# Product-key scatter on one NeuronCore: two f16 parts in one 64-column matmul, combined on three engines

## The reference, cut to what matters

```python
s, i = jax.lax.top_k(sim, k)                  # 8 best of 64 keys, for two halves x and y of the key
all_scores = (sx[..., :, None] + sy[..., None, :]).reshape(b, n, h, k * k)
all_idx = (ix[..., :, None] * nk + iy[..., None, :]).reshape(b, n, h, k * k)
scores, pk = jax.lax.top_k(all_scores, k)     # 8 best of the 64 pairs, for each of 8 heads
idx = jnp.take_along_axis(all_idx, pk, axis=-1)
o = jnp.einsum('bnd,bnhkd->bnhk', inputs, key_in[idx])
o = jax.nn.gelu(o) * jax.nn.softmax(scores, axis=-1)
return jnp.einsum('bnhk,bnhkd->bnd', o, key_out[idx])
```

## Time and profile before

| | |
|---|---|
| median of 3 runs | 3328.03 us (3327.47 to 3328.57) |
| profiled execution | 3329.2 us, its span 3327.3 us |
| TensorE busy | 3090.9 us, 93% |
| VectorE / ScalarE / GpSimd busy | 58% / 36% / 15% |
| mean granted TensorE clock | 0.959 of full speed |
| scatter matmuls L830 | 8192, 296.7 us busy |
| VectorE multiply L839 | 128, 151.9 us busy |

### The profile page before, as it was taken

One profiled execution on the slowest core, in us unless ns is written; L12 is line 12 of the kernel. 1 busy time (PEld: TensorE's weight loads), 2 busy tenths in 40 slices (PEclk: granted clock), 3 DMA queues, 4 the chain that ended last, 5 costly groups with the idle time before them and its releaser, 6 DMA issues.

```text
span 3327.3 us, 72707 instructions
## 1 busy us (share of the span) xinstructions
PE 3090.9 (93%) x28718; PEld 2424.8 (73%) x28718; DVE 1934.7 (58%) x6645; ACT 1190.9 (36%) x2696; POOL 491.6 (15%) x645
## 2 busy tenths in 40 slices
PE   7999969999999999999999999966999957999997
PEld 5578558777777777777777777634666645999996
DVE  3245457666666666666666666534676735444443
ACT  0133222333333333333333333222555532555553
POOL 0366000000000000000000000002234321333332
PEclk9999969999999999999999999977999987999998
DMA  3122430101010110101010101110122112222223
GB/s 131 43 87 88 144 137 5 33 18 33 17 33 24 27 30 21 30 21 33 17 33 17 33 18 33 32 47 1 56 83 77 43 54 82 39 36 39 36 39 77
DMA packets 89666, 153.50 MB, mean 46 GB/s; under 512 B 17152, under 2 KB 72192, under 8 KB 86176
## 3 DMA queue, kind: packets, MB, share of 16 engines
q1 hardware_dynamic: 68736, 111.50, 11.8%
q0 software_dynamic: 20448, 37.32, 5.3%
q10 hardware_dynamic: 144, 0.03, 0.0%
HBM read 100.53 MB, written 52.46 MB: 46 GB/s over the span
## 4 chain that ended last, share of the span: by engine, by line
PE 75%; DVE 5%; DMA 2%; ACT 2%; issue 1%; SPq 1%; POOL 0%; POOLq 0%; DVEq 0%; ACTq 0%
PE ps L847 14%; PE ps L670 13%; PE ps L830 8%; PE ps L908 8%; PE ps L1807 8%; PE ps L1822 7%; PE ps L881 3%; PE ps L698 2%; PE ps L699 2%; PE ps L1217 1%; PE ps L1321 1%; PE ps L1277 1%; PE ps L1342 1%; PE ps L1393 1%; PE ps L1254 1%
## 5 line engine op out<-in xcount | busy, mean ns | idle before, releaser
L670 PEld LDWEIGHTS ps<-arena 128*128 128x128 f32 x4096 | 536.8, 192 | 29.7 <-issue 2.5
L847 PE MATMUL ps<-arena 128*128 128x256 f32 x2048 | 551.7, 393 | 0.0
L670 PE MATMUL ps<-arena 128*128 128x128 f32 x4096 | 539.6, 276 | 2.0 <-ACT arena L678 2.0
L847 PEld LDWEIGHTS ps<-arena 128*128 128x128 f32 x2048 | 355.5, 190 | 161.5 <-issue 132.5
L678 ACT ACTIVATE arena<-ps 128x256 f32<-128x256 f32 x512 | 193.2, 384 | 525.8 <-PE ps L670 524.9
L929 DVE SCALAR_TENSOR_TENSOR arena<-arena 128x128 f32<-128x128 f32 x256 | 74.1, 289 | 442.1 <-ACT arena L920 442.0
L908 PE MATMUL ps<-arena 128*16 128x256 f32 x4096 | 283.1, 396 | 29.1 <-DVE arena L938 28.7
L830 PE MATMUL ps<-arena 64*128 64x32 f16 x8192 | 296.7, 245 | 1.5 <-DVE arena L818 1.5
L830 PEld LDWEIGHTS ps<-arena 64*128 64x128 f16 x8192 | 277.2, 158 | 17.9 <-DVE arena L818 2.4
L920 ACT ACTIVATE arena<-ps 128x256 f32<-128x256 f32 x256 | 97.8, 382 | 532.1 <-PE ps L908 532.1
L1549 POOL MEMSET arena<- 128x3072 f32 x1 | 2.7, 2658 | 1845.4 <-PE ps L847 1845.4
(11 more groups left out here) (272 smaller groups left out, 4768.1 us busy)
## 6 DMA issues: line engine op xcount, KB each, us to landing
xw_scratch<-arena SPq DMA_DIRECT2D x32, 512.0 KB, 2.6
arena<-xw_scratch SPq DMA_DIRECT2D x128, 128.0 KB, 4.1
arena<-in_W SPq DMA_DIRECT2D x16, 1024.0 KB, 5.2
arena<-ys_scratch SPq DMA_DIRECT2D x16, 512.0 KB, 8.7
x_scratch<-arena SPq DMA_DIRECT2D x64, 128.0 KB, 2.2
xn_scratch<-arena SPq DMA_DIRECT2D x32, 129.0 KB, 2.7
arena<-in_xT SPq DMA_DIRECT2D x8, 512.0 KB, 8.1
arena<-in_kinT SPq DMA_DIRECT2D x1, 4096.0 KB, 14.6
```

The costliest lines, as they stand in the source:

```text
L670: m = e.matmul(bank(b)[:, 128 * i:128 * i + 128], kin[:, k, 2 * jp + i, :], xcT[:, k, 128 * blk:128 * blk + 128], start=(k == 0), stop=(k ...
L847: m = e.matmul(bank(7)[:, 0:256], G[blk % 2][:, j, :], kout[:, j, :], start=(j == 0), stop=(j == 31))
```

## The change

The product of a token is one matmul of 64 columns for each half instead of two of 32: the moving operand is both planes of `Y12` side by side, and both parts land next to each other in PSUM, unsummed. A bank holds 512 words, so that a group now has 8 tokens per half: eight groups of 16 matmuls in a block (u = 0 to 7), at jp = 1, 2, 4, 6, ..., 14, each now ahead of that position's LSTM step. Summing and multiplying take three engines, for each group: ScalarE copies the upper plane from PSUM to an SBUF buffer `Wg` (two of them), VectorE adds the lower plane to it, GpSimd multiplies `G` by it. The next group's matmuls wait for the VectorE addition (`wv`), since there is one pair of banks.

```diff
-        def wgroup_tensor(e, blk, r):
-            e.wait_ge(s["xy"], 3 * n + 3)
+        def wgroup_tensor(e, blk, u):
+            n, r = 8 * blk + u, u // 2
+            e.wait_ge(s["xy"], 12 * blk + 3 * r + 3)
             if n:
-                e.wait_ge(s["A"], n)
-            for q in range(16):
-                for i in range(2):
-                    for half in range(2):
-                        p0 = 64 * half
-                        m = e.matmul(bank(4 + half)[:, 32 * q:32 * q + 32], X[b][p0:p0 + 64, :, q],
-                                     Y12[b][p0:p0 + 64, i, :, q], start=(i == 0), stop=(i == 1))
+                e.wait_ge(s["wv"], n)
+            for q in range(8):
+                for half in range(2):
+                    p0, t0 = 64 * half, 8 * (u % 2) + q
+                    m = e.matmul(bank(4 + half)[:, 64 * q:64 * q + 64], X[r % 2][p0:p0 + 64, :, t0],
+                                 Y12[r % 2][p0:p0 + 64, :, :, t0], start=True, stop=True)
             m.then_inc(s["wg"], 1)
-        def wgroup_vector(e, blk, r):
-            e.wait_ge(s["wg"], n + 1)
-            e.wait_ge(s["G"], 16 * blk + 16)
-            e.tensor_tensor(gv, gv, bank(4, 2).rearrange("p (g t j) -> p g j t", g=2, j=32), ALU.mult).then_inc(s["A"], 1)
+        def wgroup_scalar(e, blk, u):
+            n = 8 * blk + u
+            e.wait_ge(s["wg"], n + 1)
+            if n >= 2:
+                e.wait_ge(s["A"], n - 1)
+            e.activation(Wg[u % 2], planes[:, :, 0], ACT.Copy).then_inc(s["wh"], 1)
+
+        def wgroup_vector(e, blk, u):
+            e.wait_ge(s["wh"], 8 * blk + u + 1)
+            e.tensor_tensor(Wg[u % 2], Wg[u % 2], planes[:, :, 1], ALU.add).then_inc(s["wv"], 1)
+
+        def wgroup_gpsimd(e, blk, u):
+            gv = G[blk % 2].rearrange("p j (g t) -> p g t j", g=2)[:, :, 8 * u:8 * u + 8]
+            e.wait_ge(s["wv"], 8 * blk + u + 1)
+            e.tensor_tensor(gv, gv, Wg[u % 2].rearrange("p (g t) j -> p g t j", g=2), ALU.mult).then_inc(s["A"], 1)
         def outmm_tensor(e, blk, jp):
             if jp == 0:
-                e.wait_ge(s["A"], 4 * blk + 4)
+                e.wait_ge(s["A"], 8 * blk + 8)
@@ peer_tensor
                 for jp in range(16):
+                    if mid and jp in (1, 2, 4, 6, 8, 10, 12, 14):
+                        wgroup_tensor(e, i + 1, jp // 2)
                     if jp % 2 == 0:
                         for t in step_of(i, jp // 2):
                             step_tensor(e, t)
-                    if mid and jp % 4 == 1:
-                        wgroup_tensor(e, i + 1, jp // 4)
```

More of the change, by code:

```diff
@@ L640, in build @@
         Y12 = [take(2, 32, 16, dt=f16) for _ in range(2)]
-        pr, eq, io8k = take(8, 8, 8), take(16, 64, dt=f16), take(8, 64, dt=f16)
-        xn = take(2, 128)
+        pr, eq = take_at(arena.at, 8, 8, 8), take(16, 64, dt=f16)
+        io8k = take(8, 64, dt=f16)
+        xn = take_at(WORDS - 256, 2, 128)
         S8, I8, T16 = take(16, 8), take(16, 8, dt=u32), take(2, 8, 8, dt=f16)
@@ L653, in build @@
         th, hs_ = take(64), take(64)
+        Wg = [take(16, 32) for _ in range(2)]
+        planes = bank(4, 2).rearrange("p (t v j) -> p t v j", v=2, j=32)
         gtc, mm2 = take_at(route_at, 320), take_at(route_at + 320, 128)
@@ L807, in onehot_vector @@
             if n >= 2:
-                e.wait_ge(s["wg"], n - 1)
+                e.wait_ge(s["wg"], 2 * n - 2)
             if r == 0:
@@ new lines, in wgroup_vector @@
+        def wgroup_vector(e, blk, u):
[4 more added lines that the diff above has]
+            e.wait_ge(s["wv"], 8 * blk + u + 1)
+            if u == 0:
+                e.wait_ge(s["G"], 16 * blk + 16)
+            e.tensor_tensor(gv, gv, Wg[u % 2].rearrange("p (g t) j -> p g t j", g=2), ALU.mult).then_inc(s["A"], 1)
@@ L990, in peer_scalar @@
                 for k in range(8):
+                    if mid and k:
+                        wgroup_scalar(e, i + 1, k)
                     for t in step_of(i, k):
@@ L1000, in peer_scalar @@
                         x1_scalar(e, i - 1)
+                    if mid and k == 0:
+                        wgroup_scalar(e, i + 1, 0)
                     if more and k == 7:
@@ L1022, in peer_vector @@
                 for k in range(8):
+                    if mid and k:
+                        wgroup_vector(e, i + 1, k)
                     for t in step_of(i, k):
@@ L1037, in peer_vector @@
                         hidden_vector(e, t)
-                    if mid and k % 2:
-                        wgroup_vector(e, i + 1, k // 2)
+                    if mid and k == 0:
+                        wgroup_vector(e, i + 1, 0)
                     if i >= 0 and k == 7:
@@ L1067, in peer_vector, with peer_gpsimd @@
                 norm1_vector(e, 2 * k)
+        def peer_gpsimd(e):
+            for blk in range(NBLK):
+                for u in range(8):
+                    wgroup_gpsimd(e, blk, u)
         def peer_sync(e):
@@ L2006, in gpsimd @@
                 stage_end(e, k)
+            peer_gpsimd(e)
             norm_gpsimd(e)
```

3 lines of the change are left out of this document (removed).

## The result

The change makes the kernel slower: 3488.57 us (median of 4 runs, 3484.42 to 3488.85) against 3327.79 us for the kernel before beside it, a ratio of 1.048 (95% interval 1.0462 to 1.0498). The time predicted was 3403; the direction was right, the size half of what came, and the time lies above the range.

The account below looks back on a forecast made before the run. TensorE's order of work was taken as the bound. Per iteration matmuls 0.05, group 2 wait 1.45, slot 7 wait 0.5, clock 0.4 make 2.4 us; times 28 is 67, plus 8 at ends: 3328 + 75 = 3403, range 3336 to 3465.

Parts of the forecast that it names:

- the fall of the clock: TensorE's clock behind the new wait at group 2: one fall in four iterations, 1.7 us each, 0.4 us per iteration.
- GpSimd's multiply: Multiply of `G`, 128x512, eight per iteration on GpSimd: 1.2 us each, from rows at 1.92 ns a column.
- the iterations at the ends: Short iterations (i = -1, 0, 1 and 30) with less TensorE work to cover VectorE: 2 us each, 8 together.
- the wait in slot 7: Transposes behind step 7 wait for VectorE's last `rows_vector`, +9.26 less up to 0.2 against +8.66: 0.5 us.
- The column price: Matmul pair at 64 columns: 122 ns, by a line through 66 ns at 32 and 270 at 144; no gain.
- The rival "columns are free": Matmul pair stays at 66 ns up to 64 columns, TensorE saves 3.6 us per iteration: 3316; chance 0.14, nearly free included.
- The exclusion: VectorE's two-input cell operations and GpSimd's multiply exclude each other: second operation held, everything behind it 0.95 us later per slot.
- The rival without exclusion (3350): No such exclusion, or multiply slips between VectorE's operations: waits 0.5 and 0, +0.6 us per iteration; chance 0.15.
- The sign "the second cell operation still at 0.23": On VectorE, in the LSTM cell: listed among the signs that the forecast is wrong; over 1 us would show it right.
- The wait at group 2: TensorE, slot 1: one-hot ends at +6.12, wanted at +4.70; wait 1.45 us per iteration, 0.5 without exclusion.
- The rival with a multiply of 1.6 us: Slower GpSimd multiply: waits 1.85 and 0.9 us, about 3430; chance 0.18 together with more clock falls.
- the rival that had it (3440): TensorE's clock falls in each iteration, 1.7 us a fall: 3440; chance 0.18 together with slower GpSimd.

Follow-up runs that it names:

- the wait filled: Changed kernel with four 256-column matmuls, their result overwritten, ahead of group 2's wait for the one-hot; 3449.0 us.
- half groups: Kernel before with its own arithmetic, cut into eight groups of 8 tokens at the changed kernel's positions; 3413.3 us, 46.7 above the kernel before.
- multiply on VectorE: Changed kernel with the multiply of `G` on VectorE instead of GpSimd; 3415.3 us.
- columns side by side: Changed kernel with each matmul's 64 columns adjacent instead of 16 elements apart (output not the reference's); 3369.5 us.
- weights and columns side by side: Changed kernel with both the 64 columns and the 128 weight columns of each matmul adjacent (output not the reference's); 3362.7 us.
- after, token pairs: Changed kernel with `X` and `Y12` stored in pairs of tokens, weights and columns 2 elements apart; 3461.1 us, ratio 1.0286 to the kernel before.
- both repairs: Changed kernel with one-hots made one slot earlier and the multiply on VectorE; 3381.7 us, 15.1 above the kernel before.

## Why the prediction was right in kind and too small

The mechanism was right: no gain from the matmuls, and a late one-hot at group 2 made later by GpSimd. Three terms of the sum failed by their size: the fall of the clock (0.4 us per iteration put, 1.6 measured), GpSimd's multiply (1.2 us put, 1.63 measured), and the iterations at the ends (8 us put, 32 measured ahead of the first LSTM step alone). A fourth, the wait in slot 7, did not come and hid 0.5 us of this per iteration.

**The column price was right.** 1.11 us for a group was predicted by the straight line through the earlier trace rows, 1.13 came; a pair takes 126 ns where 122 was put. The rival "columns are free" is refuted. The Trainium skill (TensorE: Matmul & The Clock Gate, section Back-to-back issue gap) has one price for 1 to 64 columns; here a pair with columns 16 elements apart takes 64 ns at 32 columns and 126 at 64, so its rule doesn't hold for such columns; with adjacent columns it takes 62 ns at 32 as at 64, which agrees with it. The straight line was right for a half wrong reason: its 66 ns at 32 columns is not a column price alone, weights and columns are level there. It also left out that the clock fell in the middle of the earlier trace rows, from full to half (the windows of its two halves, about 16 matmuls each):

```profile
72.30:76.50 4.20, 4.20 (x17) 2.38 (x16) 0.00 (x0) 0.60 (x1) 0.00 (x0) 1.00 0.02 4
76.50:80.80 4.30, 4.30 (x18) 2.42 (x16) 0.00 (x0) 0.00 (x0) 0.00 (x0) 0.50 0.00 0
```

The starts are 0.27 us apart in both, so the price of these columns did not depend on the clock, and the line could be used at full clock. The changed kernel's own groups show the same: that at 510.25, one of the rows ahead of the LSTM above, ran at half clock and took 1.12 us, to 511.37, against 1.13.

```profile
510.20:511.20 1.00, 0.95 (x16) 0.92 (x16) 0.00 (x0) 0.00 (x0) 0.00 (x0) 0.50 0.00 0
```

**The exclusion was right.** With GpSimd's multiply one of the two cell operations takes 1.5 to 1.75 us in most slots, without it none is above 0.31. The rival without exclusion (3350) is refuted; the Trainium skill's rule (SBUF — State Buffer, section Who interferes with whom) holds for the three-operand form too. The prediction set that rule beside L1476, with 0.58 against 0.159 us, but L1476 reads one SBUF tile and a constant; the two-input instruction of those rows is L1480, 0.36 us beside GpSimd. What was wrong is which operation is held in slot 1: the first, not the second. The sign "the second cell operation still at 0.23" came true there without its meaning.

**The wait at group 2 was in the right place, and mis-sized by GpSimd's multiply.** Step 1 to the cell was predicted as +1.54 and is 1348.80 - 1347.26 = 1.54. The multiply was put at 1.2 us from the earlier trace rows; it takes 1.63. It also begins 0.33 us earlier than was put (+1.50 instead of +1.83), since it gets ahead of the first cell operation. That brings nothing: the first operation, held until then, and the second are both still to come behind it. So the second ends at +3.53 instead of +3.05, and the wait is 1.88 instead of 1.45 (6.12 - 4.70 of its own sum is 1.42). With a multiply of 1.63 the predicted order would have given +3.48, nearly the same; that the wrong order did no harm to the number is luck. Group 4, put at "no wait" with nothing to spare, waits 0.42. The rival with a multiply of 1.6 us gave 1.85 for group 2, which is what came, and a wait of 0.9 in slot 7, which did not; together with more falls of the clock it had been given 0.18. The error is that a multiply with steps of 128 words was priced by rows without steps, although the text had named this.

**The wait in slot 7 did not come.** Predicted 0.5, measured none. The last of `rows_vector` (L779) and the transposes that need it, from the time lines of VectorE and TensorE:

```profile
1392.61 0.28 DVE L779 COPY arena<-arena 128x128 f32<-128x128 f32 x1
```

```profile
1384.30 1.06 PE L921 MATMUL ps<-arena 128*16 128x256 f32 x16
...
1392.97 0.52 PE L791 MATMUL ps<-arena 128*128 128x128 f32 x3
```

TensorE comes at +8.67 of step 6, as predicted (8.66). VectorE ends at +8.59, not at +9.06 to 9.26. The LSTM cell began 0.5 us earlier against its step than before (+1.85 instead of +2.37), where 0.2 at most was allowed, and the reduction took 1.98 us instead of 2.21. Where the matmuls are cheaper (adjacent columns), this wait appears at once, 0.4 us each.

**The clock was the term most in error in the steady stage.** One fall in four iterations was predicted, 0.4 us per iteration; it falls in every one and costs 1.6 (slot 2 on average, against the same with the wait filled). This alone adds 1.2 us per iteration. The price of one fall was right (1.7 put), the number of falls was not. The one row with a wait, showed a fall behind 0.54 us of it, but the length of the wait alone does not tell how often it comes. Counted in the traces between 700 and 2000 us:

| kernel | wait ahead of group 2, us | iterations with a fall behind it |
|---|---|---|
| half groups | 0.45 | 0 of 24 |
| multiply on VectorE | 1.15 | 12 of 23 |
| columns side by side | 1.75 | 14 of 23 |
| after | 1.88 | 23 of 23 |
| weights and columns side by side | 1.98 | 15 of 24 |
| after, token pairs | 2.89 | 23 of 23 |

"Always" could not have been read from the one row; the rival that had it (3440) could have been given more.

The sum per iteration, predicted and measured: matmuls 0.05 and 0.05; waits 1.95 and 2.36; clock 0.4 and 1.6; together 2.4 and 4.0. The iteration is 4.5 longer. Of the missing 0.5, 0.2 is the place of group 0, to which the prediction had given 0.1: "both repairs", with neither waits nor falls, is 0.2 above 54.0. Another 0.2 stands in slot 5, 7.75 against 7.54 with early one-hots: ahead of group 6 (1383.16 in the trace) TensorE stands still for 0.13 us, too short to be listed as a wait. The last 0.1 is lost beside the two listed waits: by starts, slots 1 and 3 are 1.96 and 0.48 longer than in "both repairs", where the waits are 1.88 and 0.42.

**The ends were the term most in error in relation to its size.** 8 us for four iterations were put as an estimate. Ahead of the first LSTM step alone 32.1 are lost. TensorE has far less work in these iterations, so every second group waits for its one-hot, 3 to 4 us in the first iteration and about 2 in the next. The chain is a ring: group 2r-1, ScalarE's copy, VectorE's addition, the top-k rows behind it, the one-hots (one of them held by GpSimd's multiply), group 2r. Moving the one-hots ahead gave back 20 of the 32; the multiply on VectorE gave back 11. All waits of TensorE from 470 us to the first step are 23.4 us, against 3.5 before. The clock is lower too: 0.90 from 480 to 637 us, against 0.97 from 480 to 605 before, by which some 12 us more are lost (an estimate, 157 x 0.10 - 125 x 0.03). The two together are the 32. Between the first and last LSTM step the growth is 133.8 where 69 was predicted. Behind the last step the changed kernel is 6.1 us shorter, and no run shows why.

Summed up: of the 86 us between 3403 and 3488.6, 26 are the ends ahead of the LSTM, 65 the stage with the LSTM (the clock, the slower multiply, the order of the groups), and -6 what follows it.

## What to carry to other kernels

Before merging small matmuls, ask what sets their rate: weights and columns with a stride each have their own price, the slower sets the pair, and the cure may be the layout and not the count. A wait that a change puts ahead of TensorE can cost twice, once as a wait and once as a clock that falls behind it; here 0.45 us never did, 1.15 in half of the iterations and 1.88 in all, so give "none" and "in each" a price of their own. An operation with a new stride is to be priced with room upwards when no row has that stride. Iterations at the ends of a pipeline, where the bounding engine has little to do, are to be walked through row by row: there the chain across engines is the bound and takes every delay in full.

## What the runs showed of the hardware that was not expected

- f16 operands of TensorE 16 elements apart: loading 64x128 weights 62 ns per pair of matmuls, columns 2.0 ns each (1.9 in the earlier trace rows), the same at a clock of 1.00 and of 0.50. With weights and columns 2 elements apart a pair takes 25 ns at 32 columns, with both adjacent 29 ns at 64.
- The same wait ahead of TensorE can be followed by a fall of the clock in one iteration and not in the next: 1.15 us, 12 of 23.
- The f16 comparison on VectorE keeps its 1.22 us for 128x2048 when its operands lie in adjacent pairs; with one input in pairs 16 elements apart it takes 2.00.
- A 128x512 f32 multiply with steps of 128 words takes 1.63 us on GpSimd and 1.22 on VectorE; the addition of the same size beside it, one operand from PSUM, 0.69.
- A VectorE operation that begins 0.04 us behind GpSimd's is held to its end: 1.72 us instead of 0.29. The f16 comparison is held too, 1.63 us instead of 0.38.
